# Grouping of the ffn tiles over the steps of a transformer block kernel: 6, 0, 5, 5 instead of 5, 1, 5, 5

## The reference

```python
x = x + attention(layernorm(x))      # 16 heads of 8 channels, causal, ALiBi, softmax, projection
x = x + ffn(layernorm(x))
# ffn: a router over 8 experts (logits, RMS, softmax, top 1) gives each token one factor, and then
h = gelu(einsum('nd,edh->neh', xf, w1) + b1)       # 8 experts x 256 hidden
y = einsum('neh,ehd->ned', h, w2) + b2
out = (y * norm_g[:, None, None]).sum(axis=1)      # all experts are summed
```

## Time and profile before

| | us |
|---|---|
| median of 3 runs | 323.85 (323.07 to 324.44) |
| the profiled execution, its own time | 324.16 |
| its span, first to last instruction | 322.4 |
| PE busy | 291.8 (91%) |
| DVE busy | 190.1 (59%) |
| ACT busy | 193.9 (60%) |
| POOL busy | 76.1 (24%) |

### The profile page before, as it was taken

The page is one execution under the profiler, slowest core; times in us unless marked ns, Lnnn a source line. Parts: engine busy times, 40 slices in busy tenths (PEclk is TensorE's granted clock), DMA queues, the critical chain, the costliest instruction groups (busy, mean ns, idle before and its releaser), DMA issues.

```text
span 322.4 us, 5513 instructions
## 1 busy us (share of the span) xinstructions
PE 291.8 (91%) x1784; PEld 191.4 (59%) x1784; DVE 190.1 (59%) x788; ACT 193.9 (60%) x323; POOL 76.1 (24%) x211
## 2 busy tenths in 40 slices
PE   0638799999969999999999999999999999999993
PEld 0435465666646666667666676657667655655651
DVE  4528479778777768564777785647776711451011
ACT  6462245556447468758577397767587786525362
POOL 3349312520133055002321181020300500000120
PEclk9999999999999999999999999999999999999999
DMA  6254300130300013003000140011001000000001
GB/s 181 91 146 121 134 4 0 33 123 2 92 29 0 0 39 123 3 0 100 19 3 2 35 142 19 2 34 49 3 3 37 0 4 0 0 2 4 30 0 33
DMA packets 12524, 13.23 MB, mean 41 GB/s; under 512 B 2064, under 2 KB 9104, under 8 KB 12240
## 3 DMA queue, kind: packets, MB, share of 16 engines
q1 hardware_dynamic: 11376, 11.70, 12.0%
q0 software_dynamic: 1024, 1.05, 1.6%
q10 hardware_dynamic: 96, 0.13, 0.2%
HBM read 5.14 MB, written 1.05 MB: 19 GB/s over the span
## 4 chain that ended last, share of the span: by engine, by line
PE 81%; DVE 10%; DMA 3%; issue 2%; ACT 1%; SPq 1%; DVEq 0%; ACTq 0%
PE ffn_bank L847 17%; PE a_ring L754 12%; PE v_ring L732 12%; PE pv_bank L779 11%; PE a_ring L685 5%; PE a_ring L760 5%; PE a_ring L687 4%; PE a_ring L686 4%; DVE unused L1066 4%; PE v_ring L808 1%; DMA q_stack<-q_lo 1%; PE v_ring L685 1%; PE v_ring L741 1%; DMA q_stack<-m_lo 1%; PE v_ring L686 1%
## 5 line engine op out<-in xcount | busy, mean ns | idle before, releaser
L1066 DVE CUSTOM_DVE_ANT_0 unused<-v_ring,cst 128x512 bf16<-128x512 f32 (+3 forms) x256 | 112.1, 487 | 52.1 <-PE v_ring L732 48.0
L559 ACT ACTIVATE probs<-a_ring 128x512 f32<-128x512 f32 (+1 forms) x192 | 92.4, 526 | 67.6 <-PE a_ring L760 66.6
L732 PE MATMUL v_ring<-k_stack,q_stack 128*128 128x512 f32 (+3 forms) x256 | 88.5, 417 | 7.3 <-DMA q_stack<-q_lo 5.1
L754 PE MATMUL a_ring<-q_stack,k_stack 128*128 128x512 f32 (+3 forms) x256 | 76.6, 359 | 2.0 <-DMA q_stack<-m_lo 2.0
L847 PE MATMUL ffn_bank<-hidden,w_sb 128*128 128x512 f32 x128 | 66.3, 602 | 1.1 <-ACT ffn_T L585 0.8
L732 PEld LDWEIGHTS v_ring<-k_stack,q_stack 128*128 128x128 f32 x256 | 48.6, 206 | 27.5 <-issue 17.1
L576 ACT ACTIVATE hidden<-a_ring,cols_sb 128x512 f32<-128x512 f32 x64 | 43.4, 688 | 32.5 <-PE a_ring L687 32.0
L754 PEld LDWEIGHTS a_ring<-q_stack,k_stack 128*128 128x128 f32 x256 | 46.5, 196 | 9.5 <-issue 5.6
L760 PE MATMUL a_ring<-score_mask,ident_bf 128*128 128x128 bf16 (+1 forms) x192 | 47.9, 251 | 0.0
L779 PE MATMUL pv_bank<-probs,v_ones 128*32 128x256 f32 (+3 forms) x512 | 42.3, 440 | 0.0
L685 PE MATMUL a_ring<-zT_hi,w_hi 128*128 128x512 f32 x64 | 33.0, 516 | 0.8 <-DVEq L965 0.8
(11 more groups left out here) (110 smaller groups left out, 289.5 us busy)
## 6 DMA issues: line engine op xcount, KB each, us to landing
q_stack<-q_hi SPq DMA_DIRECT2D x8, 256.0 KB
k_stack<-k_hi SPq DMA_DIRECT2D x60, 32.0 KB
x_in<-x SPq DMA_DIRECT2D x4, 256.0 KB, 4.0
hidden<-w SPq DMA_DIRECT2D x1, 1024.0 KB, 8.3
k_stack<-k_lo POOLq DMA_DIRECT2D x32, 32.0 KB, 2.3
q_stack<-q_lo SPq DMA_DIRECT2D x4, 256.0 KB
w_sb<-w SPq DMA_DIRECT2D x1, 1024.0 KB, 5.1
x_res<-x SPq DMA_DIRECT2D x4, 256.0 KB, 3.6
```

The source lines that it names most:

```text
L559: act.activation(probs[:, n % 2, q, KIND_AT[kind]:KIND_AT[kind] + cols], a_bank()[:, 0:cols], ACT.Exp).then_inc(e_freed, 1)
L732: last = pe.matmul(dst[:, at:at + P * (n + 1)], q_stack[b % 2][:, s, n * P:(n + 1) * P], k_stack[:, s, q, 0:P * (n + 1)], start=True, stop ...
L754: pe.matmul(dst[:, at:at + P * (TB - j)], k_stack[:, s, q, j * P:(j + 1) * P], q_stack[b % 2][:, s, j * P:T], start=(at == 0), stop=False, ...
L1066: ins = dve.tensor_tensor_reduce(unused[:, (uses[0] - 1) % V_BANKS, at:at + cols], bank_[:, at:at + cols], cst[:, C_MASK + T - cols:C_MASK ...
```

## The change

Three tables for the steps change; nothing else does.

```diff
-TILES = (5, 1, 5, 5)
-LAST_TILES = (2, 2, 4)
-FFN1_AT = (1, 1, 2, 2, 4)
-FFN2_AT = (4, 7, 9, 11, 14)
+TILES = (6, 0, 5, 5)
+LAST_TILES = (4, 0, 4)
+FFN1_AT = (1, 1, 2, 2, 3, 4)
+FFN2_AT = (4, 6, 8, 10, 12, 14)
```

## The result

The changed kernel takes 325.6 us (median of 8 runs, 325.25 to 326.47), the kernel before 323.85 us beside it (8 runs, 323.07 to 324.62). The ratio is 1.0055, with an interval of 1.0041 to 1.0069. The forecast was 325.9 in 323.7 to 328.0: slower by about half a per cent, as the likeliest case had it.

A forecast was written before the change was run, and what follows sets the result against it. PE (TensorE) was taken to bound the kernel, idle 0.0 us before its score groups. Terms 0.9 + 0.6 + 0.6 - 0.1 = +2.0 us on 323.85 gave 325.9 us, range 323.7 to 328.0.

The forecast's parts named there:

- the likeliest case: The prediction's own sum of terms: 325.9 us, own range 325.0 to 327.2, chance 0.60.
- The price of a tile: On PE, ffn1 0.69 plus ffn2 0.86 us, 1.55 per tile; moving tiles between steps sums to 0.
- Table loads: On ACT, 6 loads of 1283 ns go, 7.7 us, costed at nothing because ACT's time is hidden behind PE.
- The first rival: ACT sets the pace after all: the six table loads come back to PE, 316.1 us with all; chance 0.05.
- The chain of z: Steps (2,0) and (3,0): one ffn2 less before transpose_z, PE stands at L816 for z, 0.43 us twice, +0.9 us.
- DVE against the ring: Steps (1,2) and (2,2): PE stands for a v bank that DVE frees, 0.3 us twice, +0.6 us.
- Step (3,2): Two tiles less: PE held at exponential unit 0 for negated maxima, then by DVE for a bank, +0.6 us.
- Step (3,3): ffn2 at place 6 instead of 7 may remove some of a hold on ACT's exponentials, -0.1 us.
- The rest at 0: Steps (1,1), (2,1), (3,1), (1,3), (2,3) and the a ring: costed at 0, ends -0.2 and +0.3 us.
- The small stands hardly occur: Rival: half of the 0.3 to 0.6 us gaps vanish, 323.9 to 325.3 us; chance 0.25.
- The loads of q and k: Rival: the next batch's loads in shrinking steps (b,2) end 1 us late in each of two steps, 328 us; chance 0.10.

The follow-up runs named there:

- One_table: Kernel before with the exponential in place of the gelu, so no table load remains in the steps (another ffn function): 322.89 us, 0.9969.
- z_two: Kernel before with the ffn2 of steps (b,0) at places 4, 5, 6, 8, 10, so two, not four, stand between project_y and transpose_z: 325.81 us, 1.0065.
- groups_alone: Changed kernel with the new groups, but groups of up to five tiles keep ffn2 at the old places 4, 7, 9, 11, 14: 325.2 us, 1.0048.
- One_sum: Changed kernel without L1129, DVE's second addition of the router's logits: 325.4 us, 1.0047.
- Last_3_1_4: Kernel before with LAST_TILES 3, 1, 4 instead of 2, 2, 4, one tile moved out of (3,2): 324.19 us, 1.0008.
- places_alone: Kernel before with the new places of ffn1 and ffn2, its groups of tiles unchanged: 325.12 us, 1.0042.
- last_step_places: Kernel before with the ffn2 of step (3,3) alone at places 4, 6, 8, 10: 323.73 us, 0.9990.

## Why the prediction was right

The sum was right and the kind of cause too: the forecast stands are there, at z and at a v bank that DVE frees late, the second one of (3,2) three fills earlier than forecast and the load's only likely. But some 0.8 of the 1.86 us lies at a place that the forecast doesn't have, the v bank of the router's logits (0.16 us in each of (1,2) and (2,2), about 0.5 in (3,2)), and the forecast stands of these steps are smaller in return. That the terms came out so near is in part luck.

**The price of a tile, and a sum of zero.** Right. The longer steps grew by 1.52, 1.52 and 3.08 us for 1.55, 1.55 and 3.10. The tail is unchanged.

**Table loads.** Right at nothing. The line of the gelu and that of the exponential, in the trace after:

```profile
L576 ACT ACT_TABLE_LOAD  x10: 1283/1283/1283, 93.3 to 314.3; - x10
...
L559 ACT ACT_TABLE_LOAD  x8: 1283/1283/1283, 102.2 to 265.2; - x8
```

Six loads of 24 are gone (13 and 11 before), 7.7 us of ACT, and (1,2), (2,2) and (3,2), where they were, show no gain: they are longer than the tile count makes them. One_table, with none at all, leaves the same steps as they were. The first rival, that ACT sets the pace, is refuted, and with it what the rule of the Trainium skill (ScalarE: Activation LUTs, "Table sets: the hidden batching unit") would have given here: batching by table did remove the loads, but they lay behind PE.

**The chain of z, +0.9.** The mechanism was right: slack of 0.47 us, an ffn2 of 0.86 taken from over it, a wait of L816 for z. PE stands as long as predicted: its last record before ends at 162.69 (162.46 + 0.23), and without a hold L816 starts 0.17 before that end (162.83 against 163.00, in the trace of before), at 162.52; it starts at 162.96, 0.44 us later against 0.43. But the step grows by 0.35, and z_two repeats it: 1.12 + 0.17 = 1.29 us of stand, 1.18 of step. So the term was over-sized by about 0.1 us a step. 0.08 of it is the short hold before `project_y` in the kernel before, 0.15 us from L760 to L808 (groups_alone, above), which the ffn2 moved ahead of it covers: it is 0.07 in the changed kernel and in z_two. Measured +0.71.

**DVE against the ring, +0.6.** The sum was a little low, and the place half right. Unit, bank and order were those predicted: the bank was put free 3.23 us into the step (189.19 - 185.96), it was at 3.26 (190.92 - 187.66), and PE came at 3.32. Measured 0.38 (1,2) and 0.35 (2,2), +0.73. Of a step's 0.35 only about 0.18 is the stand at this unit. PE was 0.16 us late before it, because the logits, with no ffn1 ahead of them, came too soon for their own bank, which the forecast did not look at. One_sum confirms who sets this point: with 0.2 us less on DVE the stand at the unit goes and the one at the logits stays. What the step would cost with the logits' bank free is open. That DVE might free the bank ahead of its readout's end is refuted: PE starts 0.06 us after it, in (2,2) as in (3,2).

**Step (3,2), +0.6.** The sum was near, +0.73, and the reason was half wrong. I let exponential unit 0 and its negated maxima be the first hold, 0.5 us. The first hold was the logits' v bank, which DVE frees after a unit that ran late: L827 would have come 0.47 us into the step (248.70 - 246.85 - 2 x 0.69) and came at 0.94 (251.69 - 250.75). I had looked for the bank only behind the logits. The load of the maxima was then mostly hidden by that hold: issued 0.41 us into the step as before (251.16 - 250.75; 247.26 - 246.85 in the trace of before), it would have been usable at 2.15 us by my own reading, and unit 0 started at 2.19, about 0.10 us late. In the kernel's code the unit waits for this load and for an a bank, and ACT, idle by then, had freed the bank; so the load is the likely cause, which no view shows. Whether alone it would have cost the 0.5 is open, since no kernel here gives the logits a free bank with (3,2) empty. The later, DVE-set stand was right in kind: the logits end on DVE 2.97 us into the step (253.72 - 250.75) instead of my 2.79 (249.64 - 246.85), and the unit that I had put at 4.71 without a hold (251.56 - 246.85) and at 5.30 with one came at 5.45 (256.20 - 250.75). But PE did not stand at that unit: the stand for DVE, 0.10 us, was three fills earlier, at 254.47. Last_3_1_4 shows the threshold that both arguments imply.

**Step (3,3), -0.1.** Right, -0.14, twice (places_alone, last_step_places).

**The rest at 0.** (·,3) gave 0.05 each. (2,1) held a hazard that I did not see: an ffn2 at place 14 covers DVE's work on v. The change kept it by its sixth tile; without the groups it costs 0.40 us. Had the change been the places alone, my forecast would have been low by that.

**The other rivals.** "The small stands hardly occur" failed in the sum: the steps give +1.9 for +2.0. Some of the stands were indeed smaller than forecast (0.18 for 0.3 us, 0.10 for 0.5), and the logits' bank made up for it. The loads of q and k: transfers of the trace after, 190:200 in 40 slices of 0.25 us, GB/s, and PE's first use of them:

```profile
GB/s 123 189 33 115 49 181 123 49 25 123 8 0 188 74 98 377 393 385 377 393 377 393 336 17 0 0 0 0 0 0 0 0 0 0 31 2 0 33 0 0
...
197.48 0.74 PE L732 MATMUL v_ring<-k_stack,q_stack 128*128 128x512 f32 x3
```

The queue is done with the 24th slice, at 196.0, 8.3 us into the step (194.0, 8.0; a slice is 0.25 us), and PE comes 1.5 us later, the 1.5 us to spare that I had read.

The medians say +1.75 us, the steps +1.86, the forecast +2.0.

## What to carry to other kernels

Where the leading engine has no gap, work moved between steps is free until it is the cover of something: for every step that becomes shorter, and every operation moved past the start of a chain on other engines, read how late the leading engine comes to the chain's end; that slack is the threshold. Ask it of every use of a shared bank in the step, the first one above all. Below the threshold a move is free, and beyond it each us moved costs nearly a us (z_two: 0.83 for 0.86). A busy engine's saved overhead (here table loads) is worth nothing where it isn't waited for. When a median can't resolve a change, lengths of steps cut at the same instruction can.

## What the runs showed that I had not expected

A stand of PE shows less idle time than it lasts, and a short one none: 0.27 us for 0.44 at L816, 0.28 for 0.47 at L827 in (3,2), 0.00 for 0.16 and for 0.18 in (2,2), since the records of earlier matmuls run on. "Idle 0.0" therefore didn't prove that PE had no stands in the kernel before, only no long ones; the one before `project_y` is such a stand. Steps reproduce to about 0.02 us from trace to trace, while the start of the first step scatters by 1 us and goes into every median.
